# VectorE's gather rounds and the sort's loops written out as straight programs, in a graph transformer layer

## The reference

```python
xn = _layernorm(x, axis=-1)
x = x + gnn(xn, src, dst, edge_weight) + mix(xn[None])[0]
x = x + ffn(_layernorm(x, axis=-1)[None])[0]

def gnn(X, edge_row, edge_col, edge_val):        # W 256 x 256, b 256
    msgs = edge_val[:, None] * X[edge_col]
    h = jax.ops.segment_sum(msgs, edge_row, num_segments=3125)
    return h @ W.T + b

def mix(x):   # linear attention over all nodes, 8 heads of 32
    q, k, v = split(einsum('nfc,oc->nfo', x, Wqkv), 3)
    q, k = elu(q) + 1.0, elu(k) + 1.0
    kv, ksum = einsum('nshd,nshm->nhmd', k, v), sum(k, axis=1)
    t = einsum('nlhd,nhmd,nlh->nlhm', q, kv, 1.0 / (einsum('nlhd,nhd->nlh', q, ksum) + 1e-6))
    x1 = layer_norm(t + x)
    return layer_norm(gelu(x1 @ W1.T + b1) @ W2.T + b2 + x1)

def ffn(x):   # 8 experts of 256 -> 512 -> 256, the two best by a router over the mean token
    ...
```

## Time and profile before

| | us |
|---|---|
| median of 3 runs | 1142.1 |
| the profiled execution | 1131.83 |
| its span | 1130.0 |
| PE busy | 840.1 (74%) |
| PEld busy | 617.1 (55%) |
| DVE busy | 731.2 (65%) |
| POOL busy | 573.8 (51%) |
| ACT busy | 407.7 (36%) |

### The profile page before, as it was taken

The page is one execution under the profiler, slowest core; times in us unless marked ns, Lnnn a source line. Parts: engine busy times, 40 slices in busy tenths (PEclk is TensorE's granted clock), DMA queues, the critical chain, the costliest instruction groups (busy, mean ns, idle before and its releaser), DMA issues.

```text
span 1130.0 us, 17128 instructions
## 1 busy us (share of the span) xinstructions
PE 840.1 (74%) x4284; PEld 617.1 (55%) x4284; DVE 731.2 (65%) x1970; ACT 407.7 (36%) x990; POOL 573.8 (51%) x633
## 2 busy tenths in 40 slices
PE   0586799965766666666665777777777778999997
PEld 0463688853434333444433545545555444699997
DVE  7999888832544455445445566666766668777785
ACT  0450899922222222222212322222222234667652
POOL 2282444436656666666666556566666640053442
PEclk9789899986888888888888888888888899999999
DMA  7120000013232323233333233322333370100000
GB/s 223 37 79 0 1 0 0 0 34 91 86 97 84 105 86 107 86 104 88 107 90 105 71 102 87 100 86 86 90 84 87 83 66 1 47 20 25 25 25 26
DMA packets 39131, 76.93 MB, mean 68 GB/s; under 512 B 9859, under 2 KB 22584, under 8 KB 39096
## 3 DMA queue, kind: packets, MB, share of 16 engines
q0 software_dynamic: 21312, 58.22, 19.2%
q1 hardware_dynamic: 17784, 18.29, 5.2%
HBM read 70.00 MB, written 6.48 MB: 68 GB/s over the span
## 4 chain that ended last, share of the span: by engine, by line
PE 55%; DVE 16%; issue 14%; DVEq 7%; another core or an unknown queue 6%; DMA 1%; ACT 1%; POOL 1%; SPq 0%; POOLq 0%
PE bank L1457 19%; PE bank L1621 11%; PE bank L1424 8%; DVE X L1034 4%; PE bank L1475 4%; PE bank L1544 2%; DVE SEL L1026 2%; PE bank L1481 2%; DVEq L1057 1%; DVE SC L871 1%; PE bank L1547 1%; DMA X<-in_x 1%; DVEq L1034 1%; DVEq L1012 1%
## 5 line engine op out<-in xcount | busy, mean ns | idle before, releaser
L547 POOL DMA_INDIRECT RING<-xg_rows,SIX x444 | 422.5, 952 | 271.0 <-issue 113.5
L1457 PE MATMUL bank<-RING,SEL 128*128 128x256 f32 x888 | 315.5, 474 | 207.9 <-DVE X L1034 152.3
L1034 DVE TENSOR_TENSOR X<-bank,X 128x256 f32 x444 | 188.6, 425 | 294.9 <-remote 141.2
L1457 PEld LDWEIGHTS bank<-RING,SEL 128*128 128x128 f32 x888 | 166.9, 223 | 335.9 <-issue 317.2
L1026 DVE TENSOR_SCALAR SEL<-iota,SLO,SW 128x128 f32<-128x128 f32 x444 | 161.3, 365 | 4.5 <-issue 4.4
L1424 PEld LDWEIGHTS bank<-OI,AS 128*128 128x128 f32 x832 | 97.2, 195 | 14.8 <-DVE AS L991 9.7
L1424 PE MATMUL bank<-OI,AS 128*128 128x128 f32 x832 | 97.4, 278 | 9.1 <-DVE AS L991 9.1
L535 POOL TENSOR_TENSOR AS<-LH,EPC 128x832 f32<-128x832 f32 x32 | 50.0, 1584 | 87.7 <-DVE LH L983 87.7
L627 ACT ACTIVATE LD<-iota,LANE 128x128 f32<-128x128 f32 x208 | 62.6, 388 | 41.6 <-DVE LANE L971 41.2
L664 ACT COPY XT<-bank 128x256 f32<-128x256 f32 x25 | 8.1, 375 | 175.8 <-remote 171.0
L798 ACT ACTIVATE HF<-bank,FB 128x256 f32<-128x256 f32 (+1 forms) x104 | 49.7, 478 | 37.8 <-PE bank L1621 32.0
(11 more groups left out here) (262 smaller groups left out, 1534.2 us busy)
## 6 DMA issues: line engine op xcount, KB each, us to landing
RING<-xg_rows,SIX POOLq DMA_INDIRECT x444
FW1A<-in_exp_w SPq DMA_DIRECT2D x8, 512.0 KB
X<-in_x SPq DMA_DIRECT2D x1, 3200.0 KB, 13.7
xg_rows<-XGS SPq DMA_DIRECT2D x12, 256.0 KB, 2.1
out<-YO SPq DMA_DIRECT2D x24, 128.0 KB, 1.7
FW<-in_exp_w SPq DMA_DIRECT2D x2, 512.0 KB, 4.5
QKVW<-in_qkv_wT SPq DMA_DIRECT2D x1, 768.0 KB
GW<-in_gnn_wT SPq DMA_DIRECT2D x1, 256.0 KB, 13.9
```

The costliest lines, as they stand in the source:

```text
L547: pool.indirect_dma_start(RING[:, at, :], None, xg_dram, bass.IndirectOffsetOnAxis(ap=SIX[:, c:c + 1], axis=0)).then_inc(gathered[at // HA ...
L1034: V.tensor_tensor(xt, bank[6 + s][:, 0:C], xt, ALU.add).then_inc(x_added[s], 1)
L1457: T.matmul(bank[6 + s][:, 0:C], SEL[:, k, :], RING[:, h * HAND + k, :], start=True, stop=True).then_inc(chunk_mm[s], 1)
```

## The change

Loops on four engines are written out: the Python source loops at build time, and each engine gets the instructions of all turns one after another, with the numbers that depended on the turn as constants. No arithmetic, no tile, no buffer and no wait between engines is changed.

```diff
@@ GpSimd
-            with pool.Fori(0, PAIRS) as i:
+            for i in range(PAIRS):
                 keep_xn(i, (0, 1))
...
-            with pool.Fori(0, TILES) as t:
+            for t in range(TILES):
                 pool.tensor_tensor(X[:, tile(t)], X[:, tile(t)], L2B, ALU.add).then_inc(x_biased, 1)
...
-            with pool.Fori(1, NG // 4) as i:
+            for i in range(1, NG // 4):
                 columns_and_rows(i)
@@ ScalarE
-            with act.Fori(0, PAIRS // 2 - 1) as h:
+            for h in range(PAIRS // 2 - 1):
...
-            with chain.loop(NG // 4 - 1, 2, first=1) as i:
+            for i in range(1, NG // 4):
                 sort_step(i)
@@ VectorE
-                with dve.Fori(0, tiles // UN) as n:
+                for n in range(tiles // UN):
...
-            with chain.loop(TILES // UN, UN) as n:
+            for n in range(TILES // UN):
...
-            with dve.Fori(1, TILES // UN) as n:
+            for n in range(1, TILES // UN):
...
-            with chain.loop(NG // 2, 2) as g:
+            for g in range(NG // 2):
                 slot_rank(g)
...
-            with dve.Fori(1, NG // 4) as i:
+            for i in range(1, NG // 4):
                 pair_operands(i, 0)
                 pair_operands(i, 1)
...
-            with dve.Fori(0, PAIRS) as i:
+            for i in range(PAIRS):
                 base = targets(i)
                 hand(base, i, 0)
                 hand(base, i, 1)
...
-            b_attend_n, b_x1_n, b_out_n, b_update_n = 12, 1, 2, 3
...
-            with chain.loop(PAIRS - 2, b_attend_n + b_x1_n + b_out_n + b_update_n, first=2) as i:
+            for i in range(2, PAIRS):
                 b_step(i, before=i - 2)
@@ TensorE
-            with pe.Fori(0, BEFORE) as i:
+            for i in range(BEFORE):
                 xg_tiles(i, (0, 1), (0, 1))
...
-            with pe.Fori(BEFORE, PAIRS - 1) as i:
+            for i in range(BEFORE, PAIRS - 1):
                 xg_tiles(i, (0, 1), (0, 1))
...
-            with pe.Fori(0, NG // 2) as g:
+            for g in range(NG // 2):
...
-            with pe.Fori(1, NG // 4) as i:
+            for i in range(1, NG // 4):
                 sort_step(i)
```

## The result

The changed kernel is faster, by 1.2%: 1129.8 us (median of 4 runs, 1129.09 to 1134.51) against 1143.4 (4 runs, 1140.75 to 1149.56), ratio 0.9882 with a 95% interval of 0.9833 to 0.9931. Run again in a later job it was 0.9871 (0.9832 to 0.9910). The forecast was 1140.0 in a range of 1122 to 1151: the time lies in the range, but the change was sized at 2.1 us and brought 13.6.

What follows compares the result with a forecast made beforehand. The prediction took the gather stage, with A rounds paced by gathers and their drain, as the bound. Terms -1.1 and -1.0 us sum to -2.1: 1129.7 us profiled, 1140.0 timed after carrying over 10 us; range 1122 to 1151.

Steps and rivals of the forecast that it cites:

- What bounds the kernel: Gather stage: no engine is full, the A round is set by gathers and waits, with a period of 27.33 us.
- the ring: A rounds: 18 gathers 1.255 us apart (22.6 us) and two waits (4.7 us) make the 27.33 us period.
- the hold: End of each A round: the engines wait until the burst's last gather has drained; VectorE stands idle 6.56 us.
- the sign of being right: A rounds would keep 27.2 to 27.3 us, with the gathers 1.255 us apart.
- VectorE's A rounds, -1.1 us: Freed slow slots gain almost nothing because the gathers' drain sets the release: 0.1 us for each of 11 rounds.
- Rival B: A rounds: the hold ends with VectorE's slow slots, so 4.9 us a turn, -54 us (1088; in part 1120); chance 0.13.
- the far end: A rounds: the extreme of that term's range, 11 x 4.9 = -54 us.
- VectorE's B rounds, -1.0 us: A turn costs 0.5 us ahead of the first add, but counts only in two of ten turns: 2 x 0.5.
- All other loops, 0: Statistics, one-hot, counts, ranking, sort and other engines' tiles: turns hidden behind queued work or TensorE's matmuls, price 0.
- Instruction supply, 0: Fetching VectorE's longer straight program among the gathers: priced 0, at the dearest 11.6 us.
- rival C: Gather stage: VectorE's instructions come late among the gathers, making the kernel slower; chance 0.19.
- The sum against the median: Whole kernel: -2.1 us from the profiled 1131.83 gives 1129.7; the timed runs' 10 us above it carried over to 1140.0.

Runs made afterwards that it cites:

- e0: The kernel before, unchanged, profiled a second time: median 1147.1 us, ratio 0.9993; its profiled execution took 1146.5 us.
- e2: The kernel before with only VectorE's ten looped B rounds written out: 1146.6 us, ratio 0.9979 (0.9955 to 1.0002).
- job 3: Third batch of follow-up runs, on another chip than the first two, with its own runs of the kernel before: 1006.6 us.
- e1: The kernel before with only VectorE's twelve A rounds written out: 1135.3 us, ratio 0.9884 (0.9864 to 0.9904).
- job 1: First batch of follow-up runs, e0 to e3, with its own runs of the kernel before: 1149.0 us.
- f4: The kernel before with all loops of the change written out but VectorE's A and B rounds, run on another chip: 1007.4 us, ratio 1.0002.
- e4: The kernel before with only VectorE's five loops ahead of the gather stage written out: 1130.0 us, ratio 0.9981.
- e5: The kernel before with only TensorE's four loops ahead of the gather stage written out: 1131.6 us, ratio 0.9974.
- e3: The kernel before with all loops of the change written out but VectorE's A and B rounds: 1135.1 us, ratio 0.9896 (0.9872 to 0.9920).
- job 2: Second batch of follow-up runs, e4 to e7, on the same chip as job 1, with its own runs of the kernel before: 1133.2 us.
- e7: The whole change again against the kernel before: 1118.7 us, ratio 0.9871 (0.9832 to 0.9910).
- f3: The kernel before, unchanged, profiled a third time, on another chip: 1007.9 us, ratio 1.0013.
- f1: The changed kernel with each A round put in a one-trip loop on VectorE: 1004.0 us, ratio 0.9976 to the kernel before.

## Why the prediction was right or wrong

That 1129.8 us fell into the range of 1122 to 1151 is luck. The range was that wide for the rivals; the forecast's own was 1136 to 1143, and its term for the A rounds was wrong by twelve times.

*What bounds the kernel.* Right for the shown execution and the kernel after, which keeps the ring and the hold, though with rounds of 27.4 to 29.1 us instead of the 27.2 to 27.3 named as the sign of being right. Wrong as a general account: in ten of eleven rounds of e0 and nine of eleven of e2 the add came late behind VectorE's table load, and in job 3 there was no hold.

*VectorE's A rounds, -1.1 us.* This is the step that failed. It has the right sign and was mis-sized by a factor of twelve: e1 measures -13.3 us (11.0 to 15.6), in job 1. It was taken from two seams of an execution in which the load was in time. They show what VectorE gains by being earlier still, 0.02 and 0.12 us; they can't show what it loses by one step more. The margin could be worked out: the load of the earlier trace rows starts at 516.79, 2.43 us after the last gather at 514.36, ends at 517.48, and the add comes 0.35 us later. One more 0.70 us step would have put it past the release. Rival B named this (the hold ends with VectorE's slow slots, "if only a part, 1120") and got 0.13; my reason against it, that ScalarE is released in the same moment, says nothing of an execution in which VectorE is later than that. The count of slow slots was wrong too: from the last select (510.93) to the add there are nine of 0.70 us, not 13, which would be 9.1 us in 6.56 us of idle time; it bears on the 4.9 us of rival B and of the far end, not on the -1.1.

*VectorE's B rounds, -1.0 us.* The price of a turn is right. From the last add of a round to the next first add it is 4.03 to 4.11 us before in nine of ten seams, and 3.46 or 3.47 after: 0.57 us where 0.5 was forecast. The count of seams was misread: the second add follows the first at once in rounds 15, 16, 23 and 24 of the shown trace, four of ten and not two, so by its own rule the term was -2 us. VectorE's timeline of the kernel after at a B seam, against the earlier trace rows:

```profile
743.82 0.42 DVE L1034 TENSOR_TENSOR X<-bank,X 128x256 f32 x1 [0.91 <-PE bank L1456]
...
744.45 0.42 DVE L1034 TENSOR_TENSOR X<-bank,X 128x256 f32 x1
```

The idle time ahead of the first add went from 1.49 to 0.91 us, and the second add follows at once, in all ten rounds; the forecast had it stay behind the drain in most. But the wait did not vanish: the third hand's adds now wait for the gathers (the last of them, at 713.09, after 0.77 us of a wait from outside), and rounds 14 to 24 gain 3.8 us in the two profiled executions (272.5, 268.7). That is no more than they vary anyway in job 1: 270.8 with the loop in e0, 272.6 without it in e2. The timed e2, 2.4 us with an interval from 5.2 to nothing, can't tell 3.8 from the 1.0 forecast.

*All other loops, 0.* Right for what they do themselves: in f4 1.0002, and the sort window is unchanged. Missed: in job 1 they took away the A rounds' loss, for with them VectorE's branch comes at 1.83 us or less after the last gather. How they do that is open.

*Instruction supply, 0, and rival C.* Right: seven q14 packets where there was one, and no round with a longer hold from the last gather to the first add (3.36 to 3.63 us). The two queues go with the engines that the prediction names: over the whole execution q14 has 19 packets in the kernel before, 26 in e1 and 21 in e4, where only VectorE's loops are straight, with q8 at 16 in all three; in e5, where only TensorE's are, q8 has 24 and q14 20. The chances give C 0.19, and the range leaves out a half of it, but no run shows a price for C: what the runs show is those packets and no lengthened hold. Nor could a gain come from fetches saved, with one packet in 280 us before; the gain in e1 came from the steps ahead of a blocking load.

*The sum against the median.* I carried the 10.3 us between profile and median over as if it were an offset. For the kernel before it was no offset: of all its executions that stand beside the change or in job 1 none is under 1140.2, so the shown one at 1131.8 was the exception, an execution with ten of eleven table loads in time. e0, within 1 us of its own median, has ten of eleven late. With e0 in hand the long rounds would have been plain.

*What stays open.* In job 1 the gain is the late table loads of the A rounds, by e1, e3 and the seams of four traces. In job 2 the change gains as much, and the traces there point at the B rounds, without showing why. No long execution of the kernel before beside the change itself (1143.4 us) was profiled; that its loss is that of job 1 is likely and not shown.

## What to carry to other kernels

Where the profiled execution lies much further under the median than the runs scatter, profile again before any wait is read: the loss may be in what the profile doesn't show. Read all seams and not one: the late add is there in one of eleven rounds of the lucky execution, and in ten of eleven of a typical one. Where an engine reaches its wait only just before the release, a seam with slack proves nothing; work out the margin, and count one slow step more. Loop counters, branches and register pointers ahead of a blocking load are worth writing out when they stand between the last work of a round and that load, even if they cost 0.05 us each elsewhere; in a job without the hold nothing of that gain was left in f4.

## What the runs showed of the hardware that was not expected

- VectorE's register steps take 0.70 us each in the hold of the A rounds in jobs 1 and 2, and 0.04 to 0.07 us at the same place in job 3. Of the kernel after's 429 sequencer steps in rounds 1 to 12 none takes 0.60 to 0.80 us, of the kernel before's 779 it is 66, though the address steps stand in the same stretch. Why, is open.
- The hold itself (all engines waiting until the gathers have drained) belongs to some jobs only: the kernel before took 1149 and 1133 us in two jobs on one chip, where the profiles (e0 to e7) have the hold, and 1006.6 us on another chip, where f3 has none. Whether the chip makes the difference is not shown.
- A table load of 18 registers is recorded with 1.57 us when it begins outside the hold, that of 12 for the tail with 0.86 or 0.87. Inside the hold most records are 0.00 to 0.20 us or 0.68 to 0.72; where the load ends behind the hold they are 0.82 to 0.88 or 1.54 to 1.57.
- TensorE's granted clock differs with the rounds: 0.87 of full speed over 300 to 600 us with the hold, 0.95 in f3 and 0.94 in f1 and f4 without it. At the end of a hold it stands at 0.50: windows of 0.5 us over 512 to 524 us of the shown profile read 1.00 up to 514.5, 0.50 from 515.0 to 521.5 and 1.00 from 522.0.

Not tried: issuing the table load of the next round ahead of the third hand, which would take it off the seam with or without loops.
